# A mixture-of-experts layer on one core: expert ups with the weights stationary and the rows moving, no turning of the hidden rows, silu begun after half of the ups

## The chip, the cores and the metric

One Trainium2 chip; the kernel runs on 1 of its cores. The metric is the time of one execution on the device in microseconds (us). The engines named below are TensorE (PE; its weight loads are PEld), VectorE (DVE), ScalarE (ACT), GpSimd (POOL) and SyncE (SP). Each has a sequencer that takes its instructions in order; in the profile a q behind an engine's name marks what the sequencer itself runs. L1205 is line 1205 of the kernel.

## What is computed

2048 rows x of 256 values go through a cross-attention block (causal self-attention, attention over 1601 rows of a context, a feed-forward of 1024) and then through a mixture of 8 experts, of which each row takes 2. The change is in the second part:

```python
router_logits = x @ wg.T
probs = jax.nn.softmax(router_logits, axis=-1)
topk_w, topk_idx = jax.lax.top_k(probs, TOP_K)          # TOP_K = 2
topk_w = topk_w / jnp.sum(topk_w, axis=-1, keepdims=True)
expert_w = jnp.sum(jax.nn.one_hot(topk_idx, E, dtype=x.dtype) * topk_w[..., None], axis=1)
h1 = jnp.einsum('th,eih->tei', x, w1)                    # E = 8 experts, H = 256, I = 512
h3 = jnp.einsum('th,eih->tei', x, w3)
y = jnp.einsum('tei,ehi->teh', jax.nn.silu(h1) * h3, w2)
out = jnp.einsum('te,teh->th', expert_w, y)
```

and x + out is the result. The inputs are float32.

## The kernel before

**Numbers in halves.** Values that TensorE multiplies are kept as two fp16 parts, hi and lo; `mm3` (L1201 to L1206) makes one product from three matmuls, with the parts `PARTS = ((0, 0), (0, 1), (1, 0))` of the stationary and the moving operand.

**Stages.** Attention and feed-forward fill the first 335 us. The rows that the experts need are stored in HBM (`hrow`), the routing sorts the 4096 pairs of row and expert into NJ = 39 tiles of 128 rows, each of one expert. The number of tiles is fixed; which expert a tile has is only known at run time. While the first tiles run, the routing of the later rows is still being worked out between them (the steps n = 2 to 14 in all engines' lists). All 8 experts' weights lie in SBUF by then (`ew`, in `arena`).

**One tile n.** POOL gathers its 128 rows (`gather`, L942). PE turns them by four 128x128 transposes (`x_trans`, L1531), ACT copies the result to `xT` (`x_copy`, L1002). PE reads the tile's expert into a register (`expert_of`, L1542; the register counts from there as `at`). `e_ups` makes the gate half into bank `ps[2q]` and the up half into `ps[2q+1]`, 12 matmuls of 512 columns: the turned rows stationary, the weights moving, so rows of x come out as rows. ACT takes silu of the gate bank (`silu`, L1143), DVE multiplies (`gated`, L2335), ACT rounds to hi (`act_hi`, L1002 again), DVE makes lo (`act_lo`, L2340); both go to `arow` (in `prob`). SP turns `arow` into `actT` (in `tT`) by one transposing DMA (`act_turn`, L707), and `e_downs` multiplies it with the down weights, 12 matmuls of 256 columns. DVE or ACT scales by the gate (`weighted`), POOL adds the rows to the output in HBM (`add`, an indirect DMA with add, L968).

**Order.** PE's list for a step n is: ups of n, transposes of n + 1, downs of n - 3 (BEHIND = 3). `actT` has 4 places (RING). The last tile is turned by PE (`last_turn`, L1657) with copies by ACT and DVE (L2442), not by a DMA. The names in the profile are those of the buffers: xT is in `probT`, `actT` in `tT`, `arow` in `prob`, `sil` in `w1m`, `ys` and the gathered rows in `y`.

The steps that the change and the prediction touch are in these functions:

Of the kernel before, what the change touches and what calls it, by code (L numbers as in the profile page):

```python
# [26 lines left out]
P = 128  # L27
# [12 lines left out]
TB = 4  # L40
# [43 lines left out]
def xattn_ffn_moe(nc, x, z, zT, w1, w2, wgT, we, b1, rows, out):  # L84
    with ExitStack() as ctx:
# [79 lines left out]
        arow = prob[:, 1, :].bitcast(F16).rearrange("p (s a c) -> p s a c", s=RING, a=2)  # L165
# [129 lines left out]
        def spread(p):  # L295
# [29 lines left out]
            e_x0 e_x1 e_x2 e_x3 e_a0 e_a1 e_a2 e_a3 e_xtr e_xcp e_up e_sil e_act e_ahi e_alo e_down e_y  # L325
            e_add0 e_add1 e_add2 e_add3 e_ltr e_lcp""".split()
# [252 lines left out]
        def last_bank(a):  # L579

            return ps[2 - 2 * ((NJ - 1) % 2) + a][:].bitcast(F16)[:, :CH]

# [30 lines left out]
        def _(sp):  # L613
# [87 lines left out]
            def act_turn(n):  # L701

                s = n % RING
                if n >= RING:
                    wait(sp, "e_down", n - RING + 1)
                wait(sp, "e_alo", n + 1)
                sp.dma_start_transpose(actT[:, s].rearrange("p a k c -> p (a k) c"),  # L707
                                       arow[:, s].rearrange("p a c -> p (a c)")).then_inc(sm[f"e_a{s}"], 16)

# [5 lines left out]
            for n in range(NJ):  # L715
                if n < NJ - 1:
                    act_turn(n)
                if n == 8:
                    store_x1(sp, NB - 1, range(NT - TB, NT))
                if n == H_AT:  # L720
                    store_h(sp, NB - 1)
# [276 lines left out]
        def _(act_):  # L998
# [142 lines left out]
            def silu(n, q):  # L1141
                act_.wait_ge(sm["e_up"], n + 1)
                a.activation(sil[:, q, :], ps[2 * q][:], ACT.Silu, scale=1.0 / WS).then_inc(sm["e_sil"], 1)  # L1143

            def act_hi(n, s):
                act_.wait_ge(sm["e_act"], n + 1)
                if not (isinstance(n, int) and n < RING):
                    act_.wait_ge(sm[f"e_a{s}"], 4 * (n - s))
                copy(arow[:, s, 0, :], ps[2 * (s % 2) + 1][:]).then_inc(sm["e_ahi"], 1)
# [41 lines left out]
            for n in range(E_LOOP, NJ):  # L1191
                e_step(n, n % RING, n + 1 < NJ)
            wait(act_, "e_ltr", 1)
            copy(actT[:, (NJ - 1) % RING, 0].rearrange("p k c -> p (k c)"),
                 last_bank(0)).then_inc(sm["e_lcp"], 1)
# [3 lines left out]
        def _(pe):  # L1199
# [344 lines left out]
            def e_ups(n, q):  # L1544
                at = expert[n]
                pe.wait_ge(sm["e_xcp"], n + 1)
                if not (isinstance(n, int) and n < 2):
                    pe.wait_ge(sm["e_alo"], n - 1)
                for h in range(2):
                    for k in range(KD):  # L1550
                        r = mm3(ps[2 * q + h][:], lambda a: xT[:, q, a * KD + k, :],
                                lambda b: ew[:, at + (k * 2 + h), b, :], k == 0, k == KD - 1)
                    if h == 0 and n + 1 < NJ:
                        expert_of(n + 1)
                r.then_inc(sm["e_up"], 1)

            def e_downs(n, s):
                q = s % 2
                at = expert.pop(n)
                if n < NJ - 1:  # L1560
                    pe.wait_ge(sm[f"e_a{s}"], 4 * (n - s) + 16)
                else:
                    wait(pe, "e_lcp", 2)
                if not (isinstance(n, int) and n < 2):
                    pe.wait_ge(sm["e_y"], n - 1)
                for k in range(KI):
                    r = mm3(psO[q][:, :D], lambda a: actT[:, s, a, k, :],
                            lambda b: ew[:, at + (2 * KD + k // 2), b, (k % 2) * D:(k % 2 + 1) * D],
                            k == 0, k == KI - 1)
                r.then_inc(sm["e_down"], 1)  # L1570
# [81 lines left out]
            def last_turn():  # L1652

                for a, done in enumerate(("e_ahi", "e_alo")):
                    wait(pe, done, NJ)
                    for k in range(KI):
                        r = t.transpose(last_bank(a)[:, k * P:(k + 1) * P],  # L1657
                                        arow[:, (NJ - 1) % RING, a, k * P:(k + 1) * P], ident16[:])
                    r.then_inc(sm["e_ltr"], 1)

            e_downs(NJ - 2, (NJ - 2) % RING)
            last_turn()
# [4 lines left out]
        def _(dve):  # L1667
# [665 lines left out]
            def gated(n, q):  # L2333
                dve.wait_ge(sm["e_sil"], n + 1)
                v.scalar_tensor_tensor(ps[2 * q + 1][:], ps[2 * q + 1][:], 1.0 / WS, sil[:, q, :], ALU.mult,  # L2335
                                       ALU.mult).then_inc(sm["e_act"], 1)

            def act_lo(n, s):
                dve.wait_ge(sm["e_ahi"], n + 1)
                v.tensor_tensor(arow[:, s, 1, :], ps[2 * (s % 2) + 1][:], arow[:, s, 0, :],  # L2340
                                ALU.subtract).then_inc(sm["e_alo"], 1)
# [95 lines left out]
            for n in range(E_LOOP, NJ - 1):  # L2437
# [3 lines left out]
            wait(dve, "e_ltr", 2)  # L2441
            v.tensor_copy(actT[:, (NJ - 1) % RING, 1].rearrange("p k c -> p (k c)"),  # L2442
                          last_bank(1)).then_inc(sm["e_lcp"], 1)
# [34 lines left out]
```

## Time and profile before

| | us |
|---|---|
| median of 3 runs | 529.51 |
| lowest, highest | 527.03, 531.07 |
| the profiled execution | 527.7 |
| its span, first to last instruction | 525.2 |
| mean granted clock of TensorE | 0.989 of full speed |

The profile's times count from the start of the span. Busy means that an engine, not its sequencer, was at work; matmuls overlap each other, so a busy PE can still be waiting for its sequencer, and how fast matmuls follow each other is read from their starts. In the timeline, consecutive instructions of one kind are merged into one row with their count, and the time of such a row runs to the end of its last matmul, which is later than the start of the next row.

### The profile page before, as it was taken

What the parts mean: (1) busy time and instruction counts of PE and PEld (TensorE: products, weight loads), DVE (VectorE), ACT (ScalarE), POOL (GpSimd) and SP (SyncE); (2) the same over time, 40 slices, a digit from 0 to 9 for tenths busy, and PEclk for the clock granted to TensorE, in tenths of its full rate; (3) what the DMA queues carried; (4) which work ended last, traced back from release to release, by engine and by line L of the source; (5) the groups of instructions that cost most, each with busy time, mean ns of one, the idle gap of its engine ahead of it and who ended that gap; (6) DMA issues with size and microseconds to landing.
All of it is one profiled execution on the core that took longest, in us unless ns stands there. A gap on an engine that the chain in (4) does not pass through costs nothing.

```text
span 525.2 us, 10993 instructions
## 1 busy us (share of the span) xinstructions
PE 497.2 (95%) x3686; PEld 326.1 (62%) x3686; DVE 377.1 (72%) x978; ACT 286.5 (55%) x575; POOL 277.9 (53%) x312
## 2 busy tenths in 40 slices
PE   7899999999999999999999999999999899999990
PEld 3576766656566666666666766655566555566660
DVE  6899887588878668968988999987878334344440
ACT  4556867647467745764649558654553333344420
POOL 4463213003643609993595862555755656776663
PEclk9999999999999999999999999999999999999995
DMA  8012534246887537884599680366696666788973
GB/s 278 14 32 71 170 101 116 86 103 105 149 177 123 150 78 166 141 163 154 109 198 192 126 277 2 91 122 109 103 205 99 111 119 120 124 136 120 129 89 39
DMA packets 135313, 65.60 MB, mean 125 GB/s; under 512 B 109757, under 2 KB 126590, under 8 KB 135262
## 3 DMA queue, kind: packets, MB, share of 16 engines
q1 hardware_dynamic: 127774, 54.69, 48.9%
q0 software_dynamic: 7488, 10.23, 12.0%
q8 instruction: 32, 0.52, 0.4%
q14 instruction: 19, 0.16, 0.1%
HBM read 28.19 MB, written 10.35 MB: 73 GB/s over the span
## 4 chain that ended last, share of the span: by engine, by line
PE 49%; issue 12%; DVE 12%; DMA 11%; ACT 7%; POOL 6%; POOLq 2%; SPq 1%; DVEq 0%; ACTq 0%
PE ps L1205 38%; DMA out<-y,qst 7%; POOL y L942 3%; DMA probT<-prob 3%; PE ps L1300 3%; PE ps L1302 3%; PE ps L1301 3%; ACT ps L1016 2%; DVE cmax L1744 2%; POOLq L962 2%; POOL out L968 2%; ACT tT L1002 1%; ACT prob L1015 1%; DVE ps L2335 1%; DMA stage<-we_in 1%
## 5 line engine op out<-in xcount | busy, mean ns | idle before, releaser
L1205 PE MATMUL ps<-arena,probT 128*128 128x256 f16 (+2 forms) x1092 | 180.7, 318 | 5.6 <-ACT probT L1002 2.4
L1205 PEld LDWEIGHTS ps<-arena,probT 128*128 128x128 f16 (+1 forms) x1092 | 104.4, 97 | 63.7 <-issue 12.4
L968 POOL DMA_INDIRECT out<-y,qst x39 | 63.2, 1620 | 14.1 <-issue 7.8
L1205 PE MATMUL ps<-arena,qT 128*128 128x512 f16 (+1 forms) x384 | 69.1, 332 | 1.0 <-DVE prob L1885 0.7
L1015 ACT ACTIVATE prob<-ps,nbias 128x512 f16<-128x512 f32 x64 | 39.0, 609 | 50.4 <-DVE nbias L1750 50.4
L1143 ACT ACTIVATE w1m<-ps 128x512 f32<-128x512 f32 x39 | 23.3, 598 | 75.5 <-PE ps L1205 65.1
L1205 PE MATMUL ps<-arena,tT 128*128 x468 | 57.2, 273 | 0.6 <-DVE tT L2442 0.6
L791 POOL TENSOR_TENSOR rstd<-veps,expo 128x1 f32<-128x1 f32 x16 | 9.0, 560 | 91.3 <-DVE veps L1779 91.3
L2335 DVE SCALAR_TENSOR_TENSOR ps<-ps,w1m 128x512 f32<-128x512 f32 x39 | 27.2, 697 | 39.1 <-ACT w1m L1143 33.7
L1205 PEld LDWEIGHTS ps<-arena,qT 128*128 128x128 f16 x384 | 32.5, 97 | 36.0 <-issue 1.7
L942 POOL DMA_INDIRECT y<-hrow,qst x39 | 40.4, 1035 | 24.3 <-DVE qst L2107 13.4
L1205 PE MATMUL ps<-tT 128*128 128x512 f16 (+3 forms) x234 | 48.8, 346 | 1.4 <-DVE probT L1810 0.8
L1205 PEld LDWEIGHTS ps<-arena,tT 128*128 128x128 f16 x468 | 44.2, 98 | 5.6 <-issue 0.8
L1205 PE MATMUL ps<-w2s,tT 128*128 128x256 f16 x384 | 47.0, 273 | 0.2
L1885 DVE TENSOR_TENSOR prob<-ps,prob 128x512 f16<-128x512 f32 x64 | 35.9, 570 | 14.2 <-ACT ps L1016 14.1
L1205 PEld LDWEIGHTS ps<-w2s,tT 128*128 128x128 f16 x384 | 37.2, 98 | 9.8 <-issue 0.3
L1205 PE MATMUL ps<-probT,w1m 128*128 128x512 f16 x144 | 42.8, 379 | 0.0
L1034 ACT ACTIVATE probT<-ps,shift 128x512 f16<-128x512 f32 (+1 forms) x36 | 23.9, 663 | 30.2 <-PE ps L1205 21.4
L1744 DVE TENSOR_REDUCE cmax<-ps 128x1 f32<-128x512 f32 x64 | 33.7, 565 | 5.5 <-PE ps L1205 5.1
L1300 PE MATMUL ps<-arena,probT 128*128 128x257 f16 x136 | 37.2, 274 | 0.3 <-DVE y L1820 0.3
L1016 ACT ACTIVATE ps<-ps,nbias 128x512 f32<-128x512 f32 x64 | 37.5, 586 | 0.0
L1302 PE MATMUL ps<-arena,probT 128*128 128x257 f16 x136 | 37.1, 273 | 0.0
(240 smaller groups left out, 907.1 us busy)
## 6 DMA issues: line engine op xcount, KB each, us to landing
stage<-we_in SPq DMA_DIRECT2D x33, 256.0 KB, 3.0
prob<-we_in SPq DMA_DIRECT2D x15, 256.0 KB, 4.4
xin<-x_in SPq DMA_DIRECT2D x16, 128.0 KB, 2.7
out<-y SPq DMA_DIRECT2D x16, 128.0 KB
hrow<-tT SPq DMA_DIRECT2D x4, 512.0 KB
y<-x_in SPq DMA_DIRECT2D x3, 512.0 KB, 6.9
stage<-z_in SPq DMA_DIRECT2D x4, 256.0 KB, 5.3
prob<-w_in SPq DMA_DIRECT2D x4, 256.0 KB, 3.1
```

The costliest lines, as they stand in the source:

```text
L942: g.indirect_dma_start(xg[:, n % RING, :], None, hrow[:rows_of(p), :], bass.IndirectOffsetOnAxis(ridx[:, n:n + 1], 0)).then_inc(sm[f"e_x{n ...
L968: g.indirect_dma_start(out[:rows_of(p), :], bass.IndirectOffsetOnAxis(ridx[:, n:n + 1], 0), ys[:, n % RING, :], None, compute_op=ALU.add). ...
L1015: a.activation(row_cols(q, 0, c), ps[c][:, :w], ACT.Exp, bias=nbias[:, q, :], scale=SM)
L1016: a.activation(ps[c][:, :w], ps[c][:, :w], ACT.Exp, bias=nbias[:, q, :], scale=SM, accum_out=esum[:, q, c:c + 1]).then_inc(sm["c_exp"], 1)
L1034: a.activation(p16[:, s % 4, 0, :w], ps[s % 2][:, :w], ACT.Exp, bias=shift[:], scale=SM).then_inc(sm["s_exp"], 1)
L1143: a.activation(sil[:, q, :], ps[2 * q][:], ACT.Silu, scale=1.0 / WS).then_inc(sm["e_sil"], 1)
L1205: r = t.matmul(o, lhs(a), rhs(b), start=first and n == 0, stop=last and n == 2)
L1300: t.matmul(o[:, :D + 1], hi, yvh[:, kt, :D + 1], start=kt == 0, stop=False)
L1302: r = t.matmul(o[:, :D + 1], lo, yvh[:, kt, :D + 1], start=False, stop=last)
L1744: v.tensor_reduce(cmax[:, q, c:c + 1], ps[c][:, :w], X, ALU.max).then_inc(sm[pre + "cmax"], 1)
L1885: v.tensor_tensor(row_cols(q, 1, c), ps[c][:, :w], row_cols(q, 0, c), ALU.subtract).then_inc(sm["c_lo"], 1)
L2335: v.scalar_tensor_tensor(ps[2 * q + 1][:], ps[2 * q + 1][:], 1.0 / WS, sil[:, q, :], ALU.mult, ALU.mult).then_inc(sm["e_act"], 1)
```

## The change

- Ups: the weights become the stationary operand, in slices of 128 of their 512 columns, and the turned rows the moving one. 12 matmuls of 512 columns become 48 of 128 (2 halves, 4 slices f, 2 k, 3 parts). The result comes out turned, so `gated`, `act_hi` and `act_lo` write straight into `actT`.
- `arow`, the 38 transposing DMAs of SP and the turning of the last tile by PE with its two copies are gone. `e_downs` waits for `e_alo` in place of the DMA; `act_hi` waits for the downs of tile n - 4, which SP did before. SP's two stores wait for `e_alo` on their own.
- The last matmul of the gate half raises `e_gate`, for which silu waits; `gated` waits for silu and for `e_up`.

```diff
         hT = tT[:, 6144:8192].rearrange("p (m a k c) -> p m a k c", m=TB, a=2, k=KD)
         actT = tT[:, 0:4096].rearrange("p (s a k c) -> p s a k c", s=RING, a=2, k=KI)
-        arow = prob[:, 1, :].bitcast(F16).rearrange("p (s a c) -> p s a c", s=RING, a=2)
+
+        def act_row(s, a):
+            return actT[:, s, a].rearrange("p k c -> p (k c)")
+
         xg = y[:, 0:RING, :].bitcast(F16)
         xT = ph[:, 4096:5120].rearrange("p (q b c) -> p q b c", q=2, b=2 * KD)
         sil = w1m[:, 0:2 * NI].rearrange("p (q c) -> p q c", q=2)
...
             n_yb n_u n_stat n_agg n_var n_rstd n_nrm n_gam n_cen n_x1 x2_in0 x2_in1
             m_stat m_agg m_var m_rstd m_h m_hhi m_hlo h_t h_tr h_cp h_half m_neg m_bias r_logit r_lg r_rk r_used r_dl r_exp r_val r_cho r_rank r_run
             h_out x1_out fill_out r_count r_tab r_next r_made r_listed r_list chain links_p
-            e_x0 e_x1 e_x2 e_x3 e_a0 e_a1 e_a2 e_a3 e_xtr e_xcp e_up e_sil e_act e_ahi e_alo e_down e_y
-            e_add0 e_add1 e_add2 e_add3 e_ltr e_lcp""".split()
+            e_x0 e_x1 e_x2 e_x3 e_xtr e_xcp e_gate e_up e_sil e_act e_ahi e_alo e_down e_y
+            e_add0 e_add1 e_add2 e_add3""".split()
         sm = {n: sem(n) for n in names}
...
             bank = ps[3] if p == 0 else behind([n for n in LISTS_AT if LISTS_AT[n] == p][0])
             return bank[:, :3 * (PHASES[p][2] - PHASES[p][1])]
-
-        def last_bank(a):
-
-            return ps[2 - 2 * ((NJ - 1) % 2) + a][:].bitcast(F16)[:, :CH]
         def x_bank(n):
...
                     if i in (at, at + 1):
                         store_x1(sp, j, range(j * TB + 2 * (i - at), j * TB + 2 * (i - at) + 2))
-            def act_turn(n):
-
-                s = n % RING
-                if n >= RING:
-                    wait(sp, "e_down", n - RING + 1)
-                wait(sp, "e_alo", n + 1)
-                sp.dma_start_transpose(actT[:, s].rearrange("p a k c -> p (a k) c"),
-                                       arow[:, s].rearrange("p a c -> p (a c)")).then_inc(sm[f"e_a{s}"], 16)
-
             loads(chunk_from(2), chunk_from(2) + len(CHUNK_PIECES[2]))
             for m in range(len(rest)):
                 rest_load(sp, m)
             store_x1(sp, 2, range(2 * TB, 3 * TB))
             store_h(sp, 2)
-            for n in range(NJ):
-                if n < NJ - 1:
-                    act_turn(n)
-                if n == 8:
-                    store_x1(sp, NB - 1, range(NT - TB, NT))
-                if n == H_AT:
-                    store_h(sp, NB - 1)
+            wait(sp, "e_alo", 9)
+            store_x1(sp, NB - 1, range(NT - TB, NT))
+            wait(sp, "e_alo", H_AT + 1)
+            store_h(sp, NB - 1)
             for s in range(RING):
                 wait(sp, f"e_add{s}", 16 * len(range(s, NJ, RING)))
...
                 copy(xT[:, q, :, :].rearrange("p b c -> p (b c)"), x_bank(n)).then_inc(sm["e_xcp"], 1)
             def silu(n, q):
-                act_.wait_ge(sm["e_up"], n + 1)
+                wait(act_, "e_gate", n + 1)
                 a.activation(sil[:, q, :], ps[2 * q][:], ACT.Silu, scale=1.0 / WS).then_inc(sm["e_sil"], 1)
             def act_hi(n, s):
                 act_.wait_ge(sm["e_act"], n + 1)
-                if not (isinstance(n, int) and n < RING):
-                    act_.wait_ge(sm[f"e_a{s}"], 4 * (n - s))
-                copy(arow[:, s, 0, :], ps[2 * (s % 2) + 1][:]).then_inc(sm["e_ahi"], 1)
+                if n >= RING:
+                    wait(act_, "e_down", n - RING + 1)
+                copy(act_row(s, 0), ps[2 * (s % 2) + 1][:]).then_inc(sm["e_ahi"], 1)
             def e_step(n, s, nxt=True):
...
                     h_copy(NB - 1, 0)
             for n in range(E_LOOP, NJ):
                 e_step(n, n % RING, n + 1 < NJ)
-            wait(act_, "e_ltr", 1)
-            copy(actT[:, (NJ - 1) % RING, 0].rearrange("p k c -> p (k c)"),
-                 last_bank(0)).then_inc(sm["e_lcp"], 1)
         @block.tensor
...
                 if not (isinstance(n, int) and n < 2):
                     pe.wait_ge(sm["e_alo"], n - 1)
                 for h in range(2):
-                    for k in range(KD):
-                        r = mm3(ps[2 * q + h][:], lambda a: xT[:, q, a * KD + k, :],
-                                lambda b: ew[:, at + (k * 2 + h), b, :], k == 0, k == KD - 1)
+                    for f in range(KI):
+                        for k in range(KD):
+                            r = mm3(ps[2 * q + h][:, f * P:(f + 1) * P],
+                                    lambda a: ew[:, at + (k * 2 + h), a, f * P:(f + 1) * P],
+                                    lambda b: xT[:, q, b * KD + k, :], k == 0, k == KD - 1)
+                    if h == 0:
+                        r.then_inc(sm["e_gate"], 1)
                     if h == 0 and n + 1 < NJ:
                         expert_of(n + 1)
                 r.then_inc(sm["e_up"], 1)
...
             def e_downs(n, s):
                 q = s % 2
                 at = expert.pop(n)
-                if n < NJ - 1:
-                    pe.wait_ge(sm[f"e_a{s}"], 4 * (n - s) + 16)
-                else:
-                    wait(pe, "e_lcp", 2)
+                wait(pe, "e_alo", n + 1)
                 if not (isinstance(n, int) and n < 2):
                     pe.wait_ge(sm["e_y"], n - 1)
                 for k in range(KI):
...
                 e_step(n, n % RING)
             e_ups(NJ - 1, (NJ - 1) % 2)
             e_downs(NJ - 3, (NJ - 3) % RING)
-            def last_turn():
-
-                for a, done in enumerate(("e_ahi", "e_alo")):
-                    wait(pe, done, NJ)
-                    for k in range(KI):
-                        r = t.transpose(last_bank(a)[:, k * P:(k + 1) * P],
-                                        arow[:, (NJ - 1) % RING, a, k * P:(k + 1) * P], ident16[:])
-                    r.then_inc(sm["e_ltr"], 1)
-
             e_downs(NJ - 2, (NJ - 2) % RING)
-            last_turn()
             e_downs(NJ - 1, (NJ - 1) % RING)
...
             def gated(n, q):
                 dve.wait_ge(sm["e_sil"], n + 1)
+                wait(dve, "e_up", n + 1)
                 v.scalar_tensor_tensor(ps[2 * q + 1][:], ps[2 * q + 1][:], 1.0 / WS, sil[:, q, :], ALU.mult,
                                        ALU.mult).then_inc(sm["e_act"], 1)
             def act_lo(n, s):
                 dve.wait_ge(sm["e_ahi"], n + 1)
-                v.tensor_tensor(arow[:, s, 1, :], ps[2 * (s % 2) + 1][:], arow[:, s, 0, :],
+                v.tensor_tensor(act_row(s, 1), ps[2 * (s % 2) + 1][:], act_row(s, 0),
                                 ALU.subtract).then_inc(sm["e_alo"], 1)
             def weighted(n, s):
...
                 e_step(n, n % RING)
             weighted(NJ - 4, (NJ - 4) % RING)
             e_step(NJ - 1, (NJ - 1) % RING, NJ - 3)
-            wait(dve, "e_ltr", 2)
-            v.tensor_copy(actT[:, (NJ - 1) % RING, 1].rearrange("p k c -> p (k c)"),
-                          last_bank(1)).then_inc(sm["e_lcp"], 1)
             weighted(NJ - 2, (NJ - 2) % RING)
             weighted(NJ - 1, (NJ - 1) % RING)
```

## Rows read from the trace of the kernel before

**Rows 1.** Page: busy share of each engine, and TensorE's clock in 40 slices.

```profile
PE 497.2 (95%) x3686; PEld 326.1 (62%) x3686; DVE 377.1 (72%) x978; ACT 286.5 (55%) x575; POOL 277.9 (53%) x312
...
PEclk9999999999999999999999999999999999999995
```

**Rows 2.** Stretches: us; busy us (instructions) of PE, PEld, DVE, ACT, POOL; clock; DMA.

```profile
402.00:422.00 20.00, 18.30 (x148) 11.53 (x149) 8.92 (x21) 7.33 (x13) 11.52 (x12) 1.00 0.68 116
...
482.00:502.00 20.00, 20.00 (x136) 12.29 (x135) 8.64 (x15) 7.96 (x15) 14.18 (x15) 1.00 0.88 128
```

**Rows 3.** Timeline of PE, one tile and the next: start us, us, what.

```profile
469.37 2.75 PE L1205 MATMUL ps<-arena,probT 128*128 x12
471.96 0.39 PE L1531 MATMUL ps<-ident,y 128*128 128x128 f16 x4
472.18 1.47 PE L1205 MATMUL ps<-arena,tT 128*128 x12
473.49 2.75 PE L1205 MATMUL ps<-arena,probT 128*128 x12
```

**Rows 4.** Waits from 335 to 511 us: us in total, times, longest.

```profile
ACT w1m L1143 <- PE ps L1205: 65.1, 32, 3.5
...
PEld ps L1205 <- issue: 13.2, 28, 2.0
```

**Rows 5.** By line: count, ns min/median/max, first and last start; whole span, then windows.

```profile
L1205 PEld LDWEIGHTS ps<-arena,probT x1092: 95/98/100, 116.0 to 505.9; 128*128 128x128 f16 x174, 65*128 65x128 f16 x8
...
L1205 PEldq FUSED_REGOPS  x624: 46/46/60, 335.2 to 511.1; - x156
...
L1205 PEldq FUSED_REGOPS  x16: 46/46/60, 498.1 to 501.0; - x16
...
L1205 PEldq FUSED_REGOPS  x2: 46/53/60, 498.5 to 499.3; - x2
...
L1205 PEldq FUSED_REGOPS  x8: 46/46/60, 502.4 to 503.3; - x8
```

**Rows 6.** Timeline of PE: static 8-column matmuls, each with a weight load, and the next.

```profile
345.96 0.74 PE L1205 MATMUL ps<-wgs,tT 128*128 128x8 f16 x24 [0.43 <-ACT tT L1002]
346.56 2.75 PE L1205 MATMUL ps<-arena,probT 128*128 x12
```

**Rows 7.** Timeline of ACT, then of DVE, in the tile of rows 3.

```profile
472.16 0.60 ACT L1143 ACTIVATE w1m<-ps 128x512 f32<-128x512 f32 x1 [2.16 <-PE ps L1205]
472.65 0.59 ACT L1002 ACTIVATE probT<-ps 128x512 f16<-128x512 f16 x1
473.52 0.60 ACT L1002 ACTIVATE prob<-ps 128x512 f16<-128x512 f32 x1 [0.28 <-DVE ps L2335]
...
472.79 0.70 DVE L2335 SCALAR_TENSOR_TENSOR ps<-ps,w1m 128x512 f32<-128x512 f32 x1 [2.07 <-issue]
...
474.27 0.68 DVE L2340 TENSOR_TENSOR prob<-ps,prob 128x512 f16<-128x512 f32 x1
```

**Rows 8.** Transposes of tile 1, of tile 38, the end; the turning DMAs by line.

```profile
333.94 0.39 PE L1531 MATMUL ps<-ident,y 128*128 128x128 f16 x4
...
500.93 0.39 PE L1531 MATMUL ps<-ident,y 128*128 128x128 f16 x4
...
506.37 2.78 PE L1205 MATMUL ps<-arena,tT 128*128 x24
...
510.32 1.54 PE L1205 MATMUL ps<-arena,tT 128*128 x12 [0.62 <-DVE tT L2442]
...
511.90 0.49 DVE L2349 TENSOR_SCALAR y<-ps,qst 128x256 f32<-128x256 f32 x1 [1.34 <-PE ps L1205]
...
517.01 1.55 POOL L968 DMA_INDIRECT out<-y,qst  x1 [0.16 <-issue]
...
L707 SPq DMA_TRANSPOSE tT<-prob x38: 1232/1234/2346, 342.0 to 503.9; - x38
```

**Rows 9.** The first warming matmuls, at half the clock and at full, by line.

```profile
L1261 PE MATMUL ps<-ones x13: 379/634/634, 1.9 to 8.2; 128*128 128x512 f16 x13
```

## The prediction

> **What bounds the kernel now.** First the page: TensorE (PE) is busy in 95% of the span, VectorE in 72%, and the granted clock of TensorE is full from the first slice to the last but one [rows 1]. The change touches only the expert stage, so next come the stretches of that stage. In its second half, where each tile is alone, PE is busy 18.3 of 20 us and later 20.0 of 20, always at clock 1.00 [rows 2]. A busy PE only says that matmuls overlap, so I read the starts in the timeline of PE: one tile is 4 transposes (471.96), 12 down matmuls (472.18), 12 up matmuls (473.49, the tile before: 469.37), and the ups of one tile follow those of the tile before by 4.12 us [rows 3]. The ups take 471.96 - 469.37 = 2.59 us, 12 times 0.216; the transposes 0.22; the downs 473.49 - 472.18 = 1.31. Sum 4.12: PE streams without a hole. In the waits, ScalarE's silu waits for PE, 65.1 us in all, and the weight loads have 13.2 us of idle time that ended by nothing visible, "issue" [rows 4].
>
> That "issue" leads to the part that decides here: TensorE's sequencer, which hands out the matmuls. Under the line of `mm3` it runs 624 FUSED_REGOPS, 16 for each of the 39 tiles [rows 5]. The code has 16 different expert-weight slices a tile whose place hangs on the register `at`: 2 halves x 2 k x 2 (hi, lo) = 8 in the ups, 4 k x 2 = 8 in the downs. So one register instruction is spent for every different address, hi and lo separately, though these differ by a constant only; the third matmul of an `mm3`, which uses hi again, needs none. How long one holds the sequencer: eight in a row start at 502.4 to 503.3, 0.9 / 7 = 0.129 us apart. The read of the next expert's number lies between two of them 0.8 us apart (498.5 to 499.3), so it costs 0.67 beyond one spacing. All 16 of one tile start within 498.1 to 501.0, with the last one 3.03 us [rows 5]: 16 x 0.129 = 2.06, plus 0.67, leaves 0.30 for waits and static instructions. Then the sequencer stands until the next tile's copy of x (472.65 + 0.59 = 473.24 in the cycle shown) is there [rows 7]. So of 4.12 us the sequencer works 3.03, and PE is the bound by 1.1 us.
>
> **The change part by part.** The sum is made against the profiled execution, span 525.2 and 2.5 around it, 527.7 in all; the median of the runs is 529.5, 0.3% above.
>
> Ups, the array. 12 matmuls of 512 columns become 48 of 128. The 4 transposes of a tile, 128 columns each with a weight load of its own, start 0.22 before the downs: 0.055 each [rows 3]. 48 x 0.055 = 2.66 against 2.59: +0.07 us a tile, hidden under the next item. Even an 8-column matmul with its own 128x128 load goes at (346.56 - 345.96) / 24 = 0.025 us [rows 6], so the loads as such are no bound in short runs.
>
> The rows give 0.055 us for a 128-column matmul with its load [rows 3]. Against the edit speaks the Trainium skill: "TensorE: Matmul & The Clock Gate", section "Back-to-back issue gap", says that a sustained stream of load and matmul pairs settles at about 81 ns each at 128 columns. By that the ups would be 3.9 us and the tile 5.4; the rows, in runs of 4 only, do not show it. It is taken up with the rivals.
>
> Ups, the sequencer. Now the expert's weights are the stationary side: `ew[:, at + (k*2+h), a, f*P:(f+1)*P]` has 2 h x 4 f x 2 k x 2 a = 32 different addresses a tile instead of 8. f is an offset of the same kind as hi/lo, and that one gets its own instruction before [rows 5]. So 24 more at 0.129 = +3.10 us a tile. Sequencer per tile: 40 x 0.129 + 0.67 + 0.30 = 6.13 us. That exceeds the array's 4.2. Nothing hides it: PE can only run what is handed out, the 12 new ones of each half come between the matmuls of that half, and the time in which the sequencer now stands (1.1 us) is used up. Could it begin the next ups earlier? It needs the copied x of the next tile: transposes are issued behind the ups, and transpose, its latency and the copy (471.96 to 473.24, 1.28) run beside 8 addresses of the downs (1.03 and 0.3), so the copy comes at about the same time as the sequencer is free. Period 6.1; bounds: the records last 46 or 60 ns [rows 5] and 0.129 is a mean over both kinds, so all short gives about 0.124 a piece and all long 0.138. With 0.1 of the 0.30 gone the low end is 5.9, with 0.2 of new waits the high end is 6.5.
>
> The stage. The transposes of tile 1 start at 333.94, of tile 38 at 500.93 [rows 8]: 37 periods, 167.0 us, 4.51 each. After: 37 x 6.13 = 226.8, **+59.8**. The 14.5 us by which the 37 periods now exceed 4.12 are routing matmuls, routing waits and late copies. Matmuls and late copies fit under 6.13; a wait of the sequencer for VectorE's routing does not. I take +4 (from 0 to +10, under 0.7 of them).
>
> Silu at `e_gate` and `gated` waiting for both: silu starts half an ups earlier, behind the gate's 24 matmuls. The chain silu 0.60, gated 0.70, hi 0.60, lo 0.68 [rows 7] ends three tiles before its downs, so it is worth 0 in the loop; on the last tile it hides one silu. `act_lo`'s later writes and `act_hi`'s wait for `e_down` of n-4 lie behind PE's order and cost 0.
>
> No turning: 38 transposing DMAs leave SP's queue [rows 8], nothing replaces them, and SP then only waits for the two stores. They ended long before the downs that waited for them; The DMA engines they leave are freer for gathers and scatter-adds. That is worth 0 while the sequencer bounds; were PE the bound, at most its idle time, which is 1.7 us in one stretch of 20 and 0 in another [rows 2], so 0 to 4 over the last 100 us.
>
> The end. Before, from 500.93: 24 downs, ups, 24 downs at 506.37, turning by TensorE, last 12 downs at 510.32, done 511.9 [rows 8]. After: 2.3 (16 addresses, two waits), ups 4.2, then 2.8 for gated, hi, lo with their handoffs (0.70 + 0.60 + 0.68 + 0.8), hiding the two downs, then 1.5: 10.8 against 10.9, 0. The scatter-adds, which lag now (the last issued at 517.01 though its rows were there at 512.4 [rows 8]), have caught up at the slower pace: -1.5 (0 to -3).
>
> Sum: 59.8 + 4 + 0 - 1.5 = +62.3; 527.7 + 62.3 = **590 us**.
>
> **The rivals.**
> - Other side, addresses cost nothing new: if the f offset is folded into the instruction, 16 register instructions remain, and PE stays the bound. Then 39 x 0.07 = +2.7, the last turning saves about 1.2 (the last ups end at 506.37, 2.8 later is 509.1, not 510.32), and the DMAs give back 0 to 4: 525 to 529, no change, faster at the very best. For it: nothing in the code forces a new address per f. Against: hi and lo, a constant apart, have one each now. It decides if fewer than about 9 more a tile are needed (1.1 / 0.129). Chance 0.12.
> - Weight loads that do not overlap in a long run of short matmuls. A load's own record lasts 0.098 us [rows 5]. If they were serial, ups 48 x 0.098 = 4.70, tile 4.70 + 1.53 = 6.23: 37 x 6.23 - 167 = 63.5, with the same +4 and -1.5 594. At a spacing halfway from 0.055 (0.077), tile 5.2, about 556. For it: no run of over 4 such matmuls is in the rows. Against: 24 pairs of load and 8-column matmul start 0.025 apart. Since the sequencer spaces the matmuls at 32 x 0.129 / 48 = 0.086 anyway, it matters only with addresses free. Chance 0.06. (By the rate of the Trainium skill's page named above, and free addresses, the time would be about 564.)
> - The clock falls. PE would stream 4.2 of 6.13 us, 68%. A 512-column matmul lasted 634 ns at the half clock and 379 at the full one [rows 9]; with streaming doubled a tile is twice 4.2 = 8.4 us: 37 x 8.4 - 167 = +144, about 672 us. Against: between 402 and 422, with holes of 1.7 us, the clock stayed 1.00 [rows 2]. Chance 0.03.
>
> **How the numbers follow.** Forecast 0.79, the rivals 0.12, 0.06, 0.03. Within the forecast: period 5.9 gives 37 x 5.9 - 167 = 51, with no waits and -3 at the end 575; period 6.5 with +10 gives 610. The load rival spans 556 to 594; reaching down to 565 takes in about half of it. So 565 to 612 leaves out the other side, the clock, half the load rival and a few hundredths at either end of the forecast: 0.2. A measurement of this kernel tells about 1%. Slower: 0.79 + 0.06 + 0.03 = 0.88; of the other-side rival 0.09 falls within 1% and 0.03 is faster.
>
> **What would show it.** Right: FUSED_REGOPS under `mm3`'s line rise from 624 to 39 x 40 = 1560, spaced about 0.13; transposes of successive tiles start 6.0 to 6.3 apart in the loop; up matmuls start in uneven steps of 0.055 and more, mean 0.085 to 0.09, with weight loads idle on "issue"; PE's busy share in the stage falls, clock 1.00; the 38 DMA_TRANSPOSE of the turning are gone. Wrong: 624 stays (the folded rival), or up matmuls evenly 0.08 to 0.10 apart with the sequencer ahead of them (the loads), or PEclk below 1 in the stage. If the period is right and the total not, look at waits for the routing before tile 16 and at the scatter-adds behind the last tile.

## The result, and the profile after

| | us |
|---|---|
| changed kernel, median of 4 runs | 594.59 (594.46 to 594.98) |
| kernel before, beside it on the same chip, 4 runs | 530.29 (527.03 to 531.24) |
| ratio | 1.1226, 95% interval 1.1175 to 1.1277 |
| span of the profiled execution | 592.5 (before 525.2) |

The change makes the kernel 12% slower. 590 was forecast, the range was 565 to 612. The page of the changed kernel, with the busy shares and the clock that answer to [rows 1]:

```profile
PE 550.9 (93%) x5082; PEld 404.9 (68%) x5082; DVE 378.1 (64%) x977; ACT 289.8 (49%) x574; POOL 276.6 (47%) x312
...
PEclk9999999999999999999999999999999999999997
```

PE still looks like the bound: 93% busy, at full clock. That number hides what happened. The view by line, of the changed kernel (count; ns min/median/max; first and last start; `mm3` is now on L1189, the read of the expert on L1526), shows the sequencer; the second row is a stretch of one tile:

```profile
L1189 PEldq FUSED_REGOPS  x1560: 46/46/60, 336.0 to 581.7; - x195
...
L1189 PEldq FUSED_REGOPS  x40: 46/46/60, 484.8 to 490.8; - x40
...
L1526 PEldq TENSOR_LOAD <-qst x39: 295/301/957, 334.4 to 568.2; - x39
```

1560 = 39 x 40, where [rows 5] had 624 = 39 x 16. The 40 of one tile start over 6.0 us; 16 did over 2.9. The timeline of PE of the changed kernel over that tile (start us, us, what, idle before) answers to [rows 3]:

```profile
484.70 0.39 PE L1515 MATMUL ps<-ident,y 128*128 128x128 f16 x4
484.93 1.47 PE L1189 MATMUL ps<-arena,tT 128*128 x12
486.24 2.07 PE L1189 MATMUL ps<-probT,arena 128*128 128x128 f16 x24
488.86 2.23 PE L1189 MATMUL ps<-probT,arena 128*128 128x128 f16 x24 [0.56 <-issue]
490.93 0.39 PE L1515 MATMUL ps<-ident,y 128*128 128x128 f16 x4
```

Transposes 0.23 and downs 1.31 are as before. The ups take 490.93 - 486.24 = 4.69 us instead of 2.59, with a hole of 0.56 in the middle, where the sequencer reads the next expert. 6.23 us from tile to tile instead of 4.12. The other engines show it as waiting for PE, and PE as waiting for nothing visible (waits of the changed kernel, 334 to 580 us, answering to [rows 4]):

```profile
DVE ps L2311 <- PE ps L1189: 115.1, 39, 4.8
...
PEld ps L1189 <- issue: 30.3, 54, 1.3
PE ps L1189 <- issue: 22.6, 39, 1.2
```

And the stage as a whole, by its first and last transposes and the last scatter-add (timelines, answering to [rows 8]):

```profile
334.69 0.39 PE L1515 MATMUL ps<-ident,y 128*128 128x128 f16 x4
...
571.10 0.39 PE L1515 MATMUL ps<-ident,y 128*128 128x128 f16 x4
...
584.24 1.55 POOL L955 DMA_INDIRECT out<-y,qst  x1 [0.16 <-issue]
```

### The profile page after: what moved, and what is told of

The parts are those of the page before. It is cut to its first block, busy times and chain, and to the rows that moved or that the text cites. A ratio compares the mean times of both kernels' runs of the same rounds, so it can differ in the third digit from the quotient of the medians.

```text
span 592.5 us, 14683 instructions
## 1 busy us (share of the span) xinstructions
PE 550.9 (93%) x5082; PEld 404.9 (68%) x5082; DVE 378.1 (64%) x977; ACT 289.8 (49%) x574; POOL 276.6 (47%) x312
## 4 chain that ended last, share of the span: by engine, by line
PE 52%; issue 18%; DMA 7%; POOL 7%; DVE 7%; ACT 5%; POOLq 2%; SPq 1%; DVEq 0%; ACTq 0%
PE ps L1189 42%; POOL out L955 6%; DMA probT<-prob 4%; PE ps L1284 2%; PE ps L1285 2%; PE ps L1286 2%; ACT ps L1003 2%; DVE cmax L1719 2%; POOLq L949 1%; DMA out<-y,qst 1%; ACT prob L1002 1%; DMA y<-x_in 1%; PE ps L1515 1%; DMA stage<-we_in 1%; DVE prob L1860 1%
## 5 line engine op out<-in xcount | busy, mean ns | idle before, releaser
L1189 PE MATMUL ps<-probT,arena 128*128 128x128 f16 x1872 | 162.8, 224 | 22.7 <-issue 22.4
L1189 PEld LDWEIGHTS ps<-probT,arena 128*128 x1872 | 129.1, 97 | 54.8 <-issue 29.8
L989 ACT ACTIVATE probT<-ps 128x512 f16<-128x512 f16 (+1 forms) x47 | 27.6, 596 | 95.9 <-PE ps L1515 88.2
L1189 PE MATMUL ps<-arena,probT 128*128 128x256 f16 (+1 forms) x624 | 72.1, 272 | 1.8 <-DMA probT<-prob 1.4
L1189 PE MATMUL ps<-arena,qT 128*128 128x512 f16 (+1 forms) x384 | 69.1, 332 | 1.0 <-DVE prob L1860 0.7
L1189 PEld LDWEIGHTS ps<-arena,probT 128*128 128x128 f16 (+1 forms) x624 | 59.4, 97 | 11.2 <-DMA probT<-prob 3.1
L1189 PE MATMUL ps<-arena,tT 128*128 x468 | 57.7, 273 | 0.0
L1189 PEld LDWEIGHTS ps<-arena,qT 128*128 128x128 f16 x384 | 32.5, 97 | 36.0 <-issue 1.7
L1189 PE MATMUL ps<-tT 128*128 128x512 f16 (+3 forms) x234 | 48.8, 346 | 1.4 <-DVE probT L1785 0.8
L1189 PEld LDWEIGHTS ps<-arena,tT 128*128 128x128 f16 x468 | 42.9, 97 | 6.5 <-issue 0.4
L1189 PE MATMUL ps<-w2s,tT 128*128 128x256 f16 x384 | 47.0, 273 | 0.2 <-issue 0.2
L1189 PEld LDWEIGHTS ps<-w2s,tT 128*128 128x128 f16 x384 | 37.2, 98 | 9.7 <-issue 0.4
L1189 PE MATMUL ps<-probT,w1m 128*128 128x512 f16 x144 | 42.8, 379 | 0.0
L1021 ACT ACTIVATE probT<-ps,shift 128x512 f16<-128x512 f32 (+1 forms) x36 | 23.9, 663 | 30.6 <-PE ps L1189 21.4
L989 ACT ACTIVATE tT<-ps 128x512 f16<-128x512 f32 (+1 forms) x50 | 30.6, 623 | 14.5 <-PE ps L1198 7.2
```

The source lines that it names most:

```text
L989: return a.activation(o, i, ACT.Copy)
L1021: a.activation(p16[:, s % 4, 0, :w], ps[s % 2][:, :w], ACT.Exp, bias=shift[:], scale=SM).then_inc(sm["s_exp"], 1)
L1189: r = t.matmul(o, lhs(a), rhs(b), start=first and n == 0, stop=last and n == 2)
```

## The experiments

Theory: the sequencer's address instructions (0.129 us each, one per different run-time address) set a tile's time. Rivals: weight loads that do not keep up in long runs; run-time addresses in weight loads being dear as such; the order of silu and the waits.

**1. The changed kernel with the ups at fixed places.**

```diff
             def e_ups(n, q):
-                at = expert[n]
+                at = 0
```

> The changed kernel with one edit: the ups of every tile use expert 0's weights, at places known when the kernel is built, so the ups need no address instruction (the result is not the layer's; all else, the read of the expert included, stays). If the addresses set the time: 39 x 8 = 312 FUSED_REGOPS under the line of mm3, the sequencer needs about 2.0 us a tile, PE is the bound again with up matmuls 0.055 us apart, a tile every 4.2 us and a total of 524 to 530 us. If instead weight loads do not keep up in a run of 48 matmuls (the Trainium skill's 81 ns a pair), the ups still take 3.9 us, a tile 5.4, the total about 565. If it were the orientation in some other way: no change from the 595 of the changed kernel.

Measured: 518.61 us, ratio to before 0.9772 (0.9709 to 0.9835). Timeline of PE of this run:

```profile
480.53 1.47 PE L1189 MATMUL ps<-arena,tT 128*128 x12
481.84 2.84 PE L1189 MATMUL ps<-probT,arena 128*128 128x128 f16 x48
484.52 0.39 PE L1515 MATMUL ps<-ident,y 128*128 128x128 f16 x4
```

48 matmuls with 48 weight loads in 484.52 - 481.84 = 2.68 us, 0.056 each. So weights may be the stationary side and loads do keep up in long runs. The reads of the expert are all still there (39 in this run's trace); only the 1248 addresses of the ups are gone (39 x 32; 312 FUSED_REGOPS are left), and 76 us with them. The rival by the Trainium skill's rate ("TensorE: Matmul & The Clock Gate", section "Back-to-back issue gap": 81 ns a pair) is out: this trace has 56 ns, tile after tile, and the measurement decides. The time is also 5 us below the expected band: without addresses the change would have been a gain of 2%, where that rival was priced at none. Run 7 says where it comes from.

**2. The kernel before, ups only cut in four moving slices.** x stays the stationary operand, all else as before.

```diff
                 for h in range(2):
-                    for k in range(KD):
-                        r = mm3(ps[2 * q + h][:], lambda a: xT[:, q, a * KD + k, :],
-                                lambda b: ew[:, at + (k * 2 + h), b, :], k == 0, k == KD - 1)
+                    for f in range(0, CH, 128):
+                        for k in range(KD):
+                            r = mm3(ps[2 * q + h][:, f:f + 128], lambda a: xT[:, q, a * KD + k, :],
+                                    lambda b: ew[:, at + (k * 2 + h), b, f:f + 128], k == 0, k == KD - 1)
```

> The kernel before with only the cut of the ups: rows stationary as before and weights moving, but in four slices of 128 columns, so 48 matmuls and 32 addresses a tile; the turning by DMA, the waits and silu stay. If the number of addresses sets the time: as the changed kernel, 6.1 to 6.4 us a tile, total 592 to 600 (the turning DMAs make nothing worse). If the weights as stationary operand, with a run-time address in the weight load, are what costs: 528 to 535.

Measured: 599.42 us, ratio 1.1304 (1.1231 to 1.1377). Weights are the moving side here and the loss is the same, so it is not a matter of which operand has the run-time address.

**3. The same with fixed places** (`at = 0` as in run 1).

> As the kernel with four moving slices, but the ups use expert 0's weights at fixed places (not the layer's result): 48 matmuls, no address in the ups. Addresses: 527 to 532, tile 4.2 us. Number of matmuls, or their loads, as the cost: 560 or more.

Measured: 529.36 us, ratio 0.9992 (0.9963 to 1.0021). 48 matmuls instead of 12 cost nothing that can be measured in the total; a tile takes 4.21 us here, not 4.12. Runs 2 and 3 differ in addresses alone: 70.1 us for 1248 of them.

**4. Two slices of 256 columns** (256 in place of 128 in run 2's edit): 24 addresses a tile.

> The kernel before with the ups cut in two slices of 256 columns: 24 matmuls and 16 addresses a tile in the ups, 24 with the downs. The sequencer then needs 24 x 0.129 + 0.97 = 4.07 us, just what PE needs (4.12). If the time is the larger of the two, this costs little: 2 to 8 us (the sequencer starts a tile's ups only when x is copied, and the read of the expert is at times slow), total 531 to 538. If every address adds its 0.129 on the path from the first one on: 8 x 0.129 x 39 = +40 us, 570.

Measured: 533.13 us, ratio 1.0064 (1.0033 to 1.0095), inside the band for the larger of two. Timeline of PE, then of ACT:

```profile
482.90 0.39 PE L1531 MATMUL ps<-ident,y 128*128 128x128 f16 x4
483.13 1.47 PE L1205 MATMUL ps<-arena,tT 128*128 x12
484.44 3.09 PE L1205 MATMUL ps<-arena,probT 128*128 x24
487.36 0.39 PE L1531 MATMUL ps<-ident,y 128*128 128x128 f16 x4
...
483.60 0.59 ACT L1002 ACTIVATE probT<-ps 128x512 f16<-128x512 f16 x1
```

A tile takes 4.46, not 4.12, although the sequencer's whole work (4.07) is below PE's. The ups, 487.36 - 484.44 = 2.92, are bound by their own handing out: 16 x 0.129 + 0.67 = 2.73. The sequencer can't save up its idle time, since a tile's ups are not handed out before its x is copied: in this trace the last address of the downs starts at 483.7 and the next FUSED_REGOPS at 484.2, when the copy ends (483.60 + 0.59). So a rule that fits this trace and that of the changed kernel within 0.2 us is: ups = the larger of 2.6 and what their own addresses and the read need, and then 0.22 and 1.31. By it the changed kernel has 32 x 0.129 + 0.67 = 4.80 (measured 4.69) and a period of 6.3 (measured 6.2). The total rises by 3.5 us only: from the transposes of tile 1 to those of tile 38 it is 175.3 us against 167.0, +8.3 and not 37 x 0.34, since many tiles were late before too, and the end behind them is 3.3 us shorter (21.0 against 24.3); the rest is within the spread of the runs (the kernel before alone spreads over 4 us).

**5. Silu late again in the changed kernel** (`wait(act_, "e_up", n + 1)` in place of `"e_gate"`).

> The changed kernel with silu waiting for both halves of the ups again, as before the change. If the sequencer's addresses set the time and the chain silu, gated, hi, lo ends well ahead of its downs: no change from 594.6 but for the last tile, where silu is no longer hidden (0 to +1 us). If the early silu carries part of the pace: 5 us or more slower.

Measured: 596.65 us, against 594.59 on another chip: 2.1 us, not the 0 to 1. Timelines, first ACT and the transposes of PE in the changed kernel, then in this run:

```profile
484.70 0.39 PE L1515 MATMUL ps<-ident,y 128*128 128x128 f16 x4
...
485.12 0.60 ACT L989 ACTIVATE probT<-ps 128x512 f16<-128x512 f16 x1 [2.44 <-PE ps L1515]
```

```profile
485.40 0.39 PE L1515 MATMUL ps<-ident,y 128*128 128x128 f16 x4
...
485.60 0.60 ACT L1130 ACTIVATE w1m<-ps 128x512 f32<-128x512 f32 x1 [4.33 <-PE ps L1189]
486.09 0.59 ACT L989 ACTIVATE probT<-ps 128x512 f16<-128x512 f16 x1
```

Silu stands ahead of the copy of x on ACT. Early, it is done before the transposes; late, the copy starts 0.69 us behind them instead of 0.42. A tile feels part of that 0.27: from the transposes of 17 to those of 38 it is 131.4 us instead of 129.7, 0.08 a tile. From tile 1 to 38 the traces differ by 1.4 us; the other 0.7 of the spans lies ahead of the expert stage and is not the edit's.

**6. The read of the expert in even tiles only.**

```diff
-                expert[n] = pe.value_load(tab[0:1, 0, n:n + 1], min_val=0, max_val=(NE - 1) * NP)
+                if n % 2:
+                    expert[n] = expert[n - 1]
+                else:
+                    expert[n] = pe.value_load(tab[0:1, 0, n:n + 1], min_val=0, max_val=(NE - 1) * NP)
```

> The changed kernel, but TensorE reads the expert's number for even tiles only; an odd tile uses the number of the one before (the result is not the layer's). Of the sequencer's time a tile, the read is 0.69 us (read, its fix-up, its assertion) beside 40 addresses. If the sequencer is busy all the time, 19 reads less give -13 us: 581 to 583. If the read is hidden (its wait overlapped by matmuls already handed out): under 3 us.

Measured: 539.74 us, 42 below what was expected. By line, this run:

```profile
L1189 PEldq FUSED_REGOPS  x800: 46/46/60, 336.6 to 527.2; - x160
...
L1529 PEldq TENSOR_LOAD <-qst x20: 301/304/488, 334.9 to 515.4; - x20
```

800 = 20 x 40: when two tiles share the register, the second one's 40 addresses are not worked out again. Tiles alternate between 5.2 to 5.5 and 4.21 us (transposes to transposes). It was a worse experiment than planned, since it took away reads and addresses together. To part them, odd tiles got a copy of the register:

```diff
-                    expert[n] = expert[n - 1]
+                    expert[n] = pe.snap(expert[n - 1], min_val=0, max_val=(NE - 1) * NP)
```

> As the run in which an odd tile uses the number of the tile before (539.7 us, with 800 address instructions in place of 1560: the addresses of the pair were worked out once and kept in registers). Here the odd tile's number is first copied to a register of its own, so its addresses have to be worked out anew, and only the 19 reads are saved. If that run's 55 us came from the addresses kept: 1560 FUSED_REGOPS under the line of mm3 again, and 594.6 less 19 x (0.69 - 0.1 for the copy) = 583 us. If they came from the reads: stays near 540.

Measured: 539.47 us, again with 800 FUSED_REGOPS, and the trace shows no instruction for the copy: this run parts nothing and is run 6 once more. But the trace of run 6 does part them. An even tile's ups have all 32 addresses and no read (the next read stands in the odd tile). Timeline of PE of run 6, ups of an even tile between the downs before and the transposes behind:

```profile
470.20 1.47 PE L1189 MATMUL ps<-arena,tT 128*128 x12
471.51 3.90 PE L1189 MATMUL ps<-probT,arena 128*128 128x128 f16 x48
475.25 0.39 PE L1515 MATMUL ps<-ident,y 128*128 128x128 f16 x4
```

3.74 us, where the changed kernel takes 4.69 with a read and, in its last tile, which has no next expert to read, 3.95 (573.97 to 577.92). So the read is on the path of a tile with 0.7 to 0.95 us (in run 6 some of it can be a head start of the sequencer, which has fewer addresses for the downs just before), and the 32 addresses alone take longer than the array's 2.68. In an odd tile the read has no addresses of the ups beside it, and the ups take 2.68 (467.30 to 469.98): there it is hidden.

**7. The turning DMAs put back where nobody needs them.** Run 1, with 34 transposing DMAs of 128 x 1024 fp16 at the old points, from weights into a dead buffer.

```diff
+            for n in range(4, NJ - 1):
+                ...
+                wait(sp, "e_alo", n + 1)
+                sp.dma_start_transpose(dead[:, s].rearrange("p (k c) -> p k c", c=P),
+                                       ew[:, s].rearrange("p a c -> p (a c)")).then_inc(sm[f"e_a{s}"], 16)
```

> The run with fixed ups (518.6 us, 11 us faster than the kernel before although its tiles take 4.21 and not 4.12 us) with 34 transposing DMAs of the old size added on SP's queue at the old points, from tile 4 on, reading weights and writing to a buffer that nobody reads: nothing waits for them. If the 11 us come from DMA engines that the turnings no longer load (gathers and scatter-adds land sooner): most of it is lost, 525 to 530, and tiles come late again between 400 and 460 us. If they come from the shorter way from lo to the downs: stays at 518 to 520.

Measured: 526.23 us, ratio 0.9977 (0.9945 to 1.001). 7.6 of the 11 us are gone again (5.4 between the two profiled executions) although no engine's work waits for these DMAs. Stretches of run 1, then of this run (us; busy us of PE, PEld, DVE, ACT, POOL; clock; DMA share; GB/s):

```profile
422.00:442.00 20.00, 20.00 (x308) 19.36 (x306) 8.49 (x15) 8.61 (x15) 13.20 (x14) 1.00 0.41 68
```

```profile
422.00:442.00 20.00, 16.96 (x253) 15.54 (x251) 7.83 (x14) 6.92 (x12) 12.31 (x14) 1.00 0.62 113
```

and the scatter-adds of each, run 1 first, from the view of DMA issues from 402 to 462 us (count, median us from issue to landing):

```profile
out<-y,qst POOLq DMA_INDIRECT x14, 3.9
```

```profile
out<-y,qst POOLq DMA_INDIRECT x14, 4.8
```

With the turnings on the DMA engines a scatter-add lands 0.9 us later (4.6 in the kernel before). The waits of this run in the same 60 us show how that reaches TensorE:

```profile
DVE y L2336 <- DMA out<-y,qst: 30.8, 11, 3.8
...
POOL gap L964 <- DMA out<-y,qst: 12.2, 8, 2.5
...
PE ps L1200 <- DVE tT L2327: 3.6, 5, 0.8
```

VectorE's scaling by the gate (L2336) waits until an earlier scatter-add has freed its buffer, `act_lo` (L2327) stands behind it in VectorE's list, and the ups of the tile after next wait for `act_lo`. TensorE never waits for a gather here. Between 421 and 442 four tiles in a row take 5.1 to 5.2 us instead of 4.21. In run 1 TensorE waits for nothing in this stretch.

**8. The last tile alone done the new way, in the kernel before.** Its ups have the weights stationary; no turning by TensorE, no two copies. From the edit:

```diff
-            last_turn()
             e_downs(NJ - 1, (NJ - 1) % RING)
```

> The kernel before, with only the last tile done the new way (weights stationary, no turning by TensorE, no two copies), silu as before. TensorE is done about 1.2 us earlier. If the end is set by the row of scatter-adds on GpSimd, which issue every 1.94 us and lag behind (the last at 517.01 for rows ready at 512.4): 0, ratio 0.998 to 1.002. If the end hangs on TensorE: -1.2 us, ratio 0.9975.

Measured: ratio 1.0006 (0.997 to 1.0041), 528.19 us. Timeline of the end of this run:

```profile
512.89 1.55 POOL L972 DMA_INDIRECT out<-y,qst  x1 [0.16 <-issue]
516.53 1.55 POOL L972 DMA_INDIRECT out<-y,qst  x1 [0.46 <-issue]
518.47 1.55 POOL L972 DMA_INDIRECT out<-y,qst  x1 [0.16 <-issue]
```

The end is that of the scatter-adds, as in [rows 8]: 24.4 us from the last transposes, against 24.3. What TensorE saves there is not seen.

**9. Silu late in run 1 (the edit of run 5 on top), and run 1 again beside it.**

> The run with fixed ups, but silu waits for both halves. With silu late on the changed kernel the time rose by 2 us: ScalarE then copies the turned x of the next tile 0.27 us later, and TensorE's sequencer, which had no slack, waited 0.09 us of it a tile. With the ups' addresses gone the sequencer has over 1 us of slack a tile, so if that is the way: no change from 518.6 but for the last tile's silu (0 to +0.6).

> The run with fixed ups again, on the same chip as the one with silu late, to compare the two: 517 to 521 us.

Measured: 520.70 and 518.60 us (ratios 0.9837, 0.98 to 0.9873, and 0.9798, 0.9762 to 0.9834). The expectation of 0 to 0.6 fell: 2.1 us. Nearly all loop tiles are alike (4.21). The difference lies where the routing of later rows is worked out between tiles: the periods 2 to 3, 3 to 4, 11 to 12 and 15 to 16 are together 1.7 us longer. Timelines of PE around tile 3, silu late, then early:

```profile
343.01 2.93 PE L1189 MATMUL ps<-probT,arena 128*128 128x128 f16 x48
346.42 0.74 PE L1189 MATMUL ps<-wgs,tT 128*128 128x8 f16 x24 [0.48 <-ACT tT L989]
```

```profile
342.78 2.84 PE L1189 MATMUL ps<-probT,arena 128*128 128x128 f16 x48
345.59 0.75 PE L1189 MATMUL ps<-wgs,tT 128*128 128x8 f16 x24
```

The router's matmuls (`wgs`) wait for ScalarE's copies of their rows, and those stand in ACT's queue behind the expert chain.

**10. Silu early alone, in the kernel before.**

```diff
+                    if h == 0:
+                        r.then_inc(sm["e_gate"], 1)
...
             def silu(n, q):
-                act_.wait_ge(sm["e_up"], n + 1)
+                act_.wait_ge(sm["e_gate"], n + 1)
...
                 dve.wait_ge(sm["e_sil"], n + 1)
+                wait(dve, "e_up", n + 1)
```

> The kernel before with one part of the change alone: silu begins behind the gate half, gated waits for silu and for both halves. With the ups' addresses fixed, silu late cost 2.1 us (520.7 against 518.6), nearly all of it in four tiles among which the routing is worked out (3 to 4: 6.91 against 6.31 us between the transposes, 11 to 12: 5.18 against 4.82, 15 to 16: 5.77 against 5.23, 2 to 3: 3.96 against 3.80): there TensorE waits for this chain. If that holds in the kernel before too: 1.5 to 2 us faster, 528, ratio 0.996 to 0.998, with those four tiles closer together, and the others unchanged at 4.12. If the turning DMAs, which come after the chain, hide it: 0.

Measured: 526.10 us against 528.79, ratio 0.9959 (0.9929 to 0.9988). Timelines of PE in the kernel before, then in this run, from the transposes of tile 15 to those of tile 16:

```profile
399.62 0.39 PE L1531 MATMUL ps<-ident,y 128*128 128x128 f16 x4
...
401.95 1.19 PE L1459 MATMUL ps<-xin,probT 128*128 128x66 f16 x32 [0.64 <-DVE xin L2090]
402.99 2.75 PE L1205 MATMUL ps<-arena,probT 128*128 x12
405.57 0.39 PE L1531 MATMUL ps<-ident,y 128*128 128x128 f16 x4
```

```profile
398.89 0.39 PE L1531 MATMUL ps<-ident,y 128*128 128x128 f16 x4
...
400.51 1.19 PE L1459 MATMUL ps<-xin,probT 128*128 128x66 f16 x32
401.55 2.75 PE L1205 MATMUL ps<-arena,probT 128*128 x12
404.13 0.39 PE L1531 MATMUL ps<-ident,y 128*128 128x128 f16 x4
```

5.24 us instead of 5.95: the routing matmuls (L1459) no longer wait for VectorE. Run 8, where silu is late as in the kernel before, has 5.95 here too. Of the other expected periods 2 to 3 (3.70 against 3.96) and 3 to 4 (6.45 against 6.82) are shorter, 11 to 12 is not (5.10; 5.21 before, 5.09 in run 8). These three make 1.3 us. The rest of the difference lies in periods that vary from one trace to the next with silu late as well: 10 to 11 takes 5.95 before, 5.25 here and 5.16 in run 8, and the 21 tiles from 17 to 38 take 91.2, 88.8 and 93.4 us. What part of that is the edit's is not shown. This one part of the change is a gain of 0.4%, small but clear of its interval, and the fastest correct kernel of the study.

## Why the prediction was right, step by step

- **One register instruction per different address, also for f.** Right, exactly: 1560. Runs 1 to 3 show that it is the addresses and neither the number of matmuls nor their loads.
- **0.129 us each, 40 a tile, 6.13 us.** Right in size, by its mechanism and not by luck: 21 tiles from the transposes of 17 (441.4) to those of 38 (571.1) took 6.18 us each. The chain of the argument was slightly off: it is not the whole work of the sequencer against the whole of PE's, but the ups' own handing out (run 4). For the changed kernel both give nearly the same, 6.1 and 6.3; for two slices they do not, and there the threshold of "about 9 more" is wrong: 8 more already lengthen a tile by 0.34 us. The bounds of 5.9 and 6.5 don't come out of their own terms: 40 x 0.124 + 0.67 + 0.20 is 5.83, and 40 x 0.138 + 0.67 + 0.30 + 0.20 is 6.69. The 6.18 lies inside either pair.
- **The stage, +59.8 and +4 for waits.** Measured (571.1 - 334.7) - 167.0 = +69.4, so 5.6 more. This is the term that was mis-sized, in two ways. The 37 periods hold 38 ups (period 3 to 4 has two and no downs, 9.8 us): counting them, 38 x 4.80 + 34 x 1.03 + 37 x 0.30 = 228.5 in place of 226.8. And what comes on top is 7.9 us, not 4. About half of it, 4.0, is in five periods with routing work (7 to 8, the three from 10 to 13, 15 to 16: 34.9 us together against 5 x 6.18). The forecast had routing matmuls fit under the sequencer's time and priced only waits for VectorE; but a tile's ups begin behind them (from 7 to 8 the ups start 0.7 us later, at 377.76, behind 24 routing matmuls that start at 377.15). Another 2 us are in the two periods without downs (6.31 and 6.04, where the sum has 5.10).
- **The array, 48 x 0.055 = 2.66.** Right: 2.68 in run 1 (the product is 2.64).
- **Silu early, 0 in the loop.** Wrong by 1.4 (traces) to 2.1 us (medians): it frees ScalarE for the copy of x (run 5), and where PE has time it shortens the routing tiles (runs 9 and 10). I had followed silu to the downs and not what stands behind it on ScalarE.
- **No turning, 0 while the sequencer bounds.** Consistent: run 2, which keeps the DMAs and silu late, is 4.8 us slower than the changed kernel, and silu late accounts for 1.4 to 2.1 of that; the other 3 or so are left open between the DMAs and the rest. Were PE the bound, it is worth 10.8 us with the early silu (run 3 against run 1), of which 2.1 are silu; I had bounded it at 4 by PE's idle time in the last 100 us and so priced the other-side rival at 525 to 529, where 518.6 was measured. The holes before tile 17 and the end (19.9 us from the last transposes in run 1, 24.3 before) were left out of that bound.
- **The end, -1.5.** Measured 24.3 - 21.4 = 2.9 us shorter, for the reason given: the last scatter-add is issued 1.4 us after its rows are there (582.9 to 584.24), not 4.6. TensorE's own end is 0.3 longer than before, where 0 was forecast. Run 8 confirms that TensorE's own end does not count.
- **The clock.** It stayed full (granted clock 0.995 over the changed kernel, 9 in every slice but the last), as [rows 2] suggested, at a lower rate of matmuls. That the 634 ns of [rows 9] are the half clock is not shown by the trace, which has a granted clock of 1.00 from 1.5 to 8.5 us.

Together: 525.2 + 69.4 - 2.9 + 0.7 (the stage began 0.7 later) = 592.4 of the 592.5 measured. The rise of the span is 67.3 us where 62.3 was forecast: the stage was forecast 5.6 too low, and the end, 1.4 too high, cancels part of it.

## What to carry to other kernels

When a matmul's operand lies at a place known only at run time, count the different addresses a step, not the matmuls: each is an instruction of TensorE's sequencer, and cutting 512 columns into four slices multiplies them. The profile's busy share doesn't show it, the count of register instructions and idle time ended by "issue" do. Take a bundle of changes apart before dropping it: here silu behind the gate half is by itself a gain of 0.4%, which the rest buried.

## What the runs showed of the hardware that was not expected

- Addresses worked out once stay usable: two tiles that take the expert from the same register ran 40 address instructions together, not 80 (800 in all, 539.7 us).
- An idle sequencer did not help later: with 24 addresses a tile, less work than PE's by sum, a tile was 0.34 us longer; its ups' addresses began only when the copy of x had ended (484.2).
- The read of a value into TensorE's register is on the path of a tile that is bound by addresses: ups with 32 addresses took 4.69 us with it, 3.74 (run 6) and 3.95 (last tile) without, and 2.68 with the read but without addresses.
- DMAs whose result no engine uses cost 7.6 us: scatter-adds landed 0.9 us later (3.9 to 4.8), VectorE waited for them and TensorE for VectorE.
